# Choosing experts for 29 of 32 tiles inside the last attention step, and loading the projection's weights behind the first keys

## The reference, cut to what matters

```python
x = layernorm(x + self_attention(x))             # 16 heads of 64, causal, then projection and bias
x = layernorm(x + cross_attention(x, ctx, mask)) # 16 heads of 16, 77 keys
logits = x @ Wr.T                                # 8 experts
probs = softmax(logits)
topk_scores, topk_experts = top_k(probs, 2)      # the choice
topk_scores = topk_scores / clip(topk_scores.sum(-1), 1e-9, None)
for e in range(8):                               # in order, with a capacity of 1280 tokens each
    elig = match.any(-1) & ~fallback ; pos = cumsum(elig) - 1
    kept = elig & (pos < cap) ; overflow = elig & (pos >= cap)
    y[kept tokens] += ffn_e(x) * score           # overflow goes to a ninth, fallback FFN
x = layernorm(x + y)
```

## Time and profile before

| | us |
|---|---|
| median of 3 runs | 1583.09 (1582.15 to 1584.85) |
| the profiled execution, whole | 1583.44 |
| its span, first to last instruction | 1581.7 |
| mean granted clock of TensorE | 0.957 |
| busy share of PE, DVE, ACT, POOL | 87%, 78%, 63%, 46% |

### The profile page before, as it was taken

The page is one execution under the profiler, slowest core; times in us unless marked ns, Lnnn a source line. Parts: engine busy times, 40 slices in busy tenths (PEclk is TensorE's granted clock), DMA queues, the critical chain, the costliest instruction groups (busy, mean ns, idle before and its releaser), DMA issues. The chain is left out here.

```text
span 1581.7 us, 49830 instructions
## 1 busy us (share of the span) xinstructions
PE 1382.8 (87%) x17712; PEld 1148.5 (73%) x17712; DVE 1231.6 (78%) x3309; ACT 996.9 (63%) x2381; POOL 731.2 (46%) x921
## 2 busy tenths in 40 slices
PE   3799999999999999999999999882999999999940
PEld 2577888788788878887888888651588888888830
DVE  4889999999999999999989998757555555555538
ACT  3767887788878778777878776522444444444426
POOL 2235456555564575565555634421233344334326
PEclk8899999999999999999999999995799999999985
DMA  8345444344434444443444323108411411111135
GB/s 215 106 130 155 125 130 123 107 138 126 119 95 141 126 115 118 130 124 107 135 124 122 95 81 84 31 8 364 173 55 46 154 46 50 49 49 47 47 118 215
DMA packets 138892, 178.80 MB, mean 113 GB/s; under 512 B 78782, under 2 KB 110654, under 8 KB 134176
## 3 DMA queue, kind: packets, MB, share of 16 engines
q1 hardware_dynamic: 127616, 153.71, 32.5%
q0 software_dynamic: 6816, 17.71, 3.6%
q10 hardware_dynamic: 4224, 4.19, 0.7%
HBM read 93.79 MB, written 65.93 MB: 101 GB/s over the span
## 5 line engine op out<-in xcount | busy, mean ns | idle before, releaser
L1626 PE MATMUL ps_e<-xt,wres 128*128 128x128 f16 x3408 | 354.4, 220 | 0.6 <-issue 0.6
L1626 PEld LDWEIGHTS ps_e<-xt,wres 128*128 x3408 | 287.8, 98 | 72.7 <-issue 1.1
L1682 ACT ACTIVATE act_g<-ps_e,b 128x128 f32<-128x128 f32 x568 | 162.1, 368 | 224.1 <-PE ps_e L1626 113.7
L1633 PE MATMUL ps_e<-wres,g_hi 128*128 x568 | 214.5, 379 | 1.1 <-DVE g_lo L1712 1.1
L691 ACT ACTIVATE probs<-st_k,nmax 128x128 f32<-128x128 f32 (+1 forms) x512 | 200.6, 449 | 13.7 <-DVE nmax L890 11.6
L1585 POOL DMA_INDIRECT z_scr<-e_y,dst_i x71 | 85.0, 1197 | 219.1 <-DVE e_y L1703 215.6
L890 DVE CUSTOM_DVE_ANT_0 st_k<-ps,causal 128x128 f32<-128x128 f32 (+1 forms) x512 | 160.2, 350 | 15.1 <-PE ps L419 14.0
L895 DVE TENSOR_TENSOR pt_lo<-ps,pt_hi 128x384 f16<-128x384 f32 x256 | 141.6, 553 | 17.6 <-ACT pt_hi L698 15.8
L1635 PE MATMUL ps_e<-wres,g_lo 128*128 x568 | 154.8, 273 | 0.0
L427 PE MATMUL ps<-ident,probs 128*128 128x128 f32 x768 | 131.2, 280 | 24.7 <-ACT probs L691 13.8
L1700 DVE SCALAR_TENSOR_TENSOR e_y<-ps_e,b 128x256 f32<-128x256 f32 x71 | 30.2, 425 | 156.0 <-PE ps_e L1635 151.7
(11 more groups left out here) (268 smaller groups left out, 4444.1 us busy)
## 6 DMA issues: line engine op xcount, KB each, us to landing
st_p<-in_moe_w SPq DMA_DIRECT2D x24, 768.0 KB, 5.7
w_scr<-st_p SPq DMA_DIRECT2D x24, 768.0 KB, 4.1
wres<-w_scr SPq DMA_DIRECT2D x18, 1024.0 KB, 19.6
v_scr<-v_tok SPq DMA_DIRECT2D x32, 512.0 KB, 2.6
v_pos<-v_scr SPq DMA_DIRECT2D x32, 512.0 KB, 4.4
k_pair<-k_pair SPq DMA_DIRECT2D x32, 512.0 KB, 4.6
z_scr<-zero SPq DMA_DIRECT2D x32, 256.0 KB, 3.5
wres<-z_scr SPq DMA_DIRECT2D x8, 1024.0 KB, 13.1
```

The lines of the kernel that those rows point to most:

```text
L1626: last = mm(out, w(c * FF + f * P, b, P), xt[:, t % 2, a, c], start=(m == 0), stop=(m == 5))
L1633: mm(out[:, 0:2 * D], g_hi[:, t % G_BUFS, f], w(KC * FF + f * D, 0, 2 * D), start=(f == 0), stop=False, skip_group_check=True)
L1682: nc.scalar.activation(act_g[:, k % 2, f], ps[:, 3 + 2 * (k % 2) + f // 4, (f % 4) * P:(f % 4 + 1) * P], ACT.Gelu, bias=bias[:, f:f + 1], ...
```

## The change

Two edits. The first splits the choice of experts. Logits of tiles 0 to 28 (`EARLY` = 29) exist before step 31; their softmax, their two best experts and their shares are now computed in step 31, at three places of DVE's order (with one `exp` on ACT, and an `iota` on POOL in step 30). The routing block does the same for the last three tiles only, its shares after the packed list, and its `free` is a memset while ACT computes the exponentials. The second takes the projection's two transfers out of `other_weights` and issues them in step -1, after `key_double(0)`; accordingly the 16 pieces of the projection are split after the 8 of the cross-attention, and PE waits for all 24 where it waited for the 24th anyway. Two buffers (`x2_up`, `y2`) move into a staging tile that has become free, and `hot` is allocated earlier.

```diff
+EARLY = TILES - 3
+class Choice:
+    def softmax_in(self, v, link):
+        link(v.tensor_reduce(self.mx, self.lg, AX.X, ALU.max))
+        return v.tensor_tensor(self.pr, self.lg, self.wide(self.mx), ALU.subtract)
+    def softmax_out(self, v, link):
+        link(v.tensor_reduce(self.sm, self.ex, AX.X, ALU.add))
+        link(v.reciprocal(self.mx, self.sm))
+        link(v.tensor_tensor(self.pr, self.ex, self.wide(self.mx), ALU.mult))
+    def best(self, v, link, k):
+        link(v.tensor_reduce(self.m[k], self.pr, AX.X, ALU.max))
+        link(v.tensor_tensor(self.tmp, self.pr, self.wide(self.m[k]), ALU.is_lt))
+        link(v.scalar_tensor_tensor(out=self.tmp, in0=self.tmp, scalar=100.0, in1=ie, op0=ALU.mult, op1=ALU.add))
+        link(v.tensor_reduce(self.ix, self.tmp, AX.X, ALU.min))
+        link(v.tensor_tensor(self.hot[k], ie, self.wide(self.ix), ALU.is_equal))
+        if k == 0:
+            link(v.scalar_tensor_tensor(out=self.pr, in0=self.hot[0], scalar=-4.0, in1=self.pr, op0=ALU.mult, op1=ALU.add))
+    def shares(self, v, link):
+        link(v.tensor_tensor(self.sm, self.m[0], self.m[1], ALU.add))
+        link(v.tensor_scalar(self.sm, self.sm, 1e-9, None, ALU.max))
+        link(v.reciprocal(self.mx, self.sm))
+        for k in range(2):
+            link(v.tensor_tensor(self.w[k], self.m[k], self.mx, ALU.mult))
...
-    SPLITS.append(("p", ld["p"], 32, stage_p[:], [wp[:, k] for k in range(2)], WP_UP))
     for n in ("k", "v", "q", "o"):
         SPLITS.append(("x" + n, ld["x"], 64, stage_x[n][:], [w2[n][:, k] for k in range(2)], WA_UP))
+    SPLITS.append(("p", ld["p"], 32, stage_p[:], [wp[:, k] for k in range(2)], WP_UP))
...
         def other_weights():
-            for half in range(2):
-                sp.dma_start(stage_p[half * HS:(half + 1) * HS], io["proj"].rearrange("(h d) n -> d h n", d=HS)).then_inc(ld["p"], 16)
...
+        def projection():
+            for half in range(2):
+                sp.dma_start(stage_p[half * HS:(half + 1) * HS], io["proj"].rearrange("(h d) n -> d h n", d=HS)).then_inc(ld["p"], 16)
...
                 key_double(s + 1)
+                if s == -1:
+                    projection()
...
-                    pe.wait_ge(s_lo, splits_until("xo"))
+                    pe.wait_ge(s_lo, splits_until("p"))
...
             if has(s - 1):
+                if s == TILES - 1:
+                    act.wait_ge(s_neg, N_SHIFTED)
+                    nc.scalar.activation(early.ex, early.pr, ACT.Exp).then_inc(s_one, 1)
                 stage_c(s - 1, 1)
...
+                if s == TILES - 1:
+                    early_softmax()
                 stage_c(s - 1, 1)
...
+                if s == TILES - 1:
+                    early_best(0)
                 stage_c(s - 1, 3)
...
+                if s == TILES - 1:
+                    early_best(1)
                 stage_c(s - 1, 5)
...
+        def early_softmax():
+            dve.wait_ge(s_lgc, EARLY)
+            link(early.softmax_in(nc.vector, link))
+            dve.wait_ge(s_one, 3)
+            early.softmax_out(nc.vector, link)
+        def early_best(k):
+            dve.wait_ge(s_const, N_CONST + 1)
+            early.best(nc.vector, link, k)
+            if k == 1:
+                early.shares(nc.vector, link)
...
+        late.softmax_in(v, link).then_inc(s_shift, 1)
+        link(v.memset(free[:], 1.0))
         dve.wait_ge(s_exp, 1)
...
+        late.softmax_out(v, link)
         dve.wait_ge(s_const, 10 + PACK)
         for k in range(2):
...
+            late.best(v, link, k)
...
         link(v.tensor_copy(te_pack_i[:], te_pack[:]))
+        late.shares(v, link)
```

More of the change, by code:

```diff
@@ L59, with __init__, wide @@
 K_OPS = OPS_BEFORE[4]
+EARLY = TILES - 3
+class Choice:
+    def __init__(self, lg, hot, w, ex, pr, tmp, mx, sm, m, ix, iota_e):
+        self.lg, self.hot, self.w, self.ex, self.pr, self.tmp = lg, hot, w, ex, pr, tmp
+        self.mx, self.sm, self.m, self.ix, self.iota_e = mx, sm, m, ix, iota_e
+        self.n = lg.shape[1]
+    def wide(self, a):
+        return a.unsqueeze(2).to_broadcast([P, self.n, E])
+    def softmax_in(self, v, link):
[6 more added lines that the diff above has]
+    def best(self, v, link, k):
+        ie = self.iota_e.unsqueeze(1).to_broadcast([P, self.n, E])
+        link(v.tensor_reduce(self.m[k], self.pr, AX.X, ALU.max))
[11 more added lines that the diff above has]
+            link(v.tensor_tensor(self.w[k], self.m[k], self.mx, ALU.mult))
 def attention_block(nc, ctx, io, keep):
@@ L122, in attention_block @@
     ctx_up = sb("ctx_up", [P, KC, CTX], F32)
-    x2_up = sb("x2_up", [P, D], F32)
     x_nat = sb("x_nat", [P, 2, D], F32)
@@ L141, in attention_block @@
     y1 = sb("y1", [P, D], F32)
-    y2 = sb("y2", [P, D], F32)
     stats = sb("stats", [P, 2, 6], F32)
@@ L171, in attention_block @@
     x2_t = stage["v"][:, 0, 0:KC * P].rearrange("p (c t) -> p c t", c=KC)
+    x2_up, y2 = (stage["v"][:, 0, n * D:(n + 1) * D] for n in (1, 2))
     logits = keep["logits"]
@@ L221, in even, with early_rows @@
         return t % 2 == 0
+    N_SHIFTED = 4
+    def early_rows(name, row, at):
+        return stage[name][:, row, at:at + EARLY * E].rearrange("p (t e) -> p t e", e=E)
+    row = stage["v"][:, 1]
+    small = [row[:, 640 + n * TILES:640 + n * TILES + EARLY] for n in range(5)]
+    iota_early = row[:, 640 + 5 * TILES:640 + 5 * TILES + E]
+    early = Choice(logits[:, 0:EARLY * E].rearrange("p (t e) -> p t e", e=E), [keep["hot"][:, k, 0:EARLY] for k in range(2)],
+                   [keep["weights"][:, k, 0:EARLY] for k in range(2)], early_rows("q", 0, 640), early_rows("q", 1, 640), early_rows("k", 0, 768),
+                   small[0], small[1], small[2:4], small[4], iota_early)
     def own(t, cc):
@@ L987, in stage_d @@
                 dve.wait_ge(s_proj2, t + 1)
-                stt(out=y2[:], in0=c7[:, 0:D], scalar=1.0 / (QK_UP * WA_UP), in1=x1[:, p], op0=ALU.mult,
+                stt(out=y2, in0=c7[:, 0:D], scalar=1.0 / (QK_UP * WA_UP), in1=x1[:, p], op0=ALU.mult,
                     op1=ALU.add).then_inc(s_y2, 1)
@@ L999, in second_norm @@
                 dve.wait_ge(s_x2_lo, t - 1)
-            nc.vector.tensor_scalar(x2[:, p], y2[:], mv[:, 1, 0:1], rstd[:, 1:2], ALU.subtract, ALU.mult).then_inc(s_x2, 1)
+            nc.vector.tensor_scalar(x2[:, p], y2, mv[:, 1, 0:1], rstd[:, 1:2], ALU.subtract, ALU.mult).then_inc(s_x2, 1)
         def step(s):
@@ L1107, in fill_own, with link @@
             dve.wait_ge(s_neg, 2)
+        linked = [2]
+        def link(ins):
+            linked[0] += 1
+            ins.then_inc(s_neg, 1)
+            dve.wait_ge(s_neg, linked[0])
+        def early_softmax():
[8 more added lines that the diff above has]
+                early.shares(nc.vector, link)
         nc.vector.memset(sm[:], NEG2).then_inc(s_neg, 1)
@@ L1168, in split_x2 @@
                 pool.wait_ge(s_out_pair[p], 16 * half(t))
-            split(pool, x2[:, p], x2_up[:], x2_pair[:, p, 0], x2_pair[:, p, 1], t, s_x2_hi, s_x2_lo)
+            split(pool, x2[:, p], x2_up, x2_pair[:, p, 0], x2_pair[:, p, 1], t, s_x2_hi, s_x2_lo)
         def split_context(b):
@@ L1250, in _, with number_experts @@
         pool.sem_inc(s_w_lo, 1)
-        run(step, {-1: constants})
+        def number_experts():
+            pool.wait_ge(s_lo, FIRST)
+            nc.gpsimd.iota(iota_early, pattern=[[1, E]], base=0, channel_multiplier=0, allow_small_or_imprecise_dtypes=True).then_inc(s_const, 1)
+        run(step, {-1: constants, TILES - 2: number_experts})
 def weight_rows(io):
@@ L1307, in routing_block @@
     one_row = sb("one_row", [P, T], F32)
[L1308 to L1312, removed]
+    L = T - EARLY
+    mx, sm, ix = (sb("r_" + n, [P, L], F32) for n in ("mx", "sm", "ix"))
+    ex, pr = (sb("r_" + n, [P, L, E], F32) for n in ("ex", "pr"))
+    m = sb("r_m", [P, 2, L], F32)
     tmp = sb("r_tmp", [P, T, E], F32)
-    ix = sb("r_ix", [P, 2, T], F32)
     both = sb("r_both", [P, E, T], F32)
@@ L1326, in routing_block @@
     sk = sb("r_sk", [P, 2, T], F32)
-    w = keep["weights"]
+    late = Choice(lg[:, EARLY:T], [hot[:, k, EARLY:T] for k in range(2)], [keep["weights"][:, k, EARLY:T] for k in range(2)],
+                  ex[:], pr[:], tmp[:, 0:L], mx[:], sm[:], [m[:, k] for k in range(2)], ix[:], iota_e[:])
     si = sb("r_si", [P, 2, T], I32)
@@ L1395, in _ @@
         act.wait_ge(s_shift, 1)
-        nc.scalar.activation(ex[:].rearrange("p t e -> p (t e)"), pr[:].rearrange("p t e -> p (t e)"), ACT.Exp).then_inc(s_exp, 1)
+        nc.scalar.activation(late.ex, late.pr, ACT.Exp).then_inc(s_exp, 1)
         act.wait_ge(s_const, 10 + PACK)
@@ L1433, in wide @@
             return a.unsqueeze(2).to_broadcast([P, T, n])
-        link(v.tensor_reduce(mx[:], lg, AX.X, ALU.max))
-        v.tensor_tensor(pr[:], lg, wide(mx[:]), ALU.subtract).then_inc(s_shift, 1)
+        late.softmax_in(v, link).then_inc(s_shift, 1)
+        link(v.memset(free[:], 1.0))
         dve.wait_ge(s_exp, 1)
```

(9 more changed lines are left out.)

## The result

| | before | changed |
|---|---|---|
| median, runs of one session | 1582.31 us (20 runs) | 1585.28 us (20 runs) |
| ratio, 95% interval | | 1.002 (1.0011 to 1.0028) |
| span of the profiled execution | 1581.7 us | 1584.9 us |
| mean granted clock | 0.957 | 0.959 |
| first scores on PE | 37.81 | 33.10 |

The change made the kernel 3 us slower, where 1.6 us faster was forecast; the time lies just outside the range of 1577 to 1585. The second half of the table (places in the two profiled executions, in us) says where: 4.7 us ahead at the first scores, 3.0 after step 0, 2.4 when step 31 begins, 3.8 behind when the routing begins, 2.5 behind at the experts.

What follows compares the result with a forecast made beforehand. The prediction took PE, then DVE, as fullest on average, with DMA limiting the experts' start. Its terms, -6.2 - 0.3 + 6.0 + 1.0 - 2.1 = -1.6 us, from the median 1583.09 gave 1581.5 us, range 1577 to 1585.

Steps and rivals of the forecast that it cites:

- Step 31, the operations: Step 31: softmax +0.6, best expert +2.6, second best and shares +2.8, together 6.0 us longer (bounds 3 and 7).
- the softmax: Step 31: nothing on DVE, but POOL's `k_bd` and the variance of tile 30 come later, +0.6 us.
- Step 31, the clock: Step 31: two holes of about 2.8 us in PE's work may lower its clock, +1.0 us, between 0 and 3.
- Rival (c): Step 31: clock falls and stays low into step 32, step 31 costs 10.5 in place of 7, total 1585; chance 0.17.
- The start: Before step 0: first keys' doubling issued 6.2 us earlier, -6.2 us, and -0.3 for PE's clock.
- the doubling: Start: transfer of the first keys, issued at 24.33 in place of 30.56, still taking 7.1 us, landing at 31.4.
- the clock term of -0.3: Start: PE resumes at 31.5, just where its clock fell, so -0.3 us taken between 0 and -1.5.
- Rival (d): Start: projection's weights land late, each us beyond 43.9 costs one us of ACT, at 47 total 1584.6; chance 0.08.
- The experts: Routing to experts: choice 3.9 us in place of 9.0, but DMA of weights and biases limits the gain to -2.1 us.
- Rival (a): Step 31: added DVE operations are covered, +2 in place of +7, total 1576.5; chance 0.17.
- (b): Routing to experts: DMA is not next, b2 lands sooner, all 5.3 us count, total 1578.3; chance 0.08.

Runs made afterwards that it cites:

- e1: Kernel before with only the projection's move and the order of its splits, no early choice: 1578.12 us, ratio 0.9968.
- e6: Kernel before with the projection's move, SP waiting for the first keys' doubling to land before asking for the projection's 2 MB: 1580.60 us, ratio 0.999.
- e9: Kernel before with the projection's move and 14 useless matmuls on PE ahead of its wait for the first keys' doubling: 1577.32 us, ratio 0.9969.
- e11: Kernel before with the projection's move alone, repeated on another chip: 1577.60 us, ratio 0.997.
- e2: Changed kernel with the projection's move taken back, so the choice of experts alone: 1589.44 us, ratio 1.0046.
- e4: Changed kernel with the ninth expert's 2.1 MB asked for behind b1 and b2, PE waiting for them only at the ninth expert tile: 1582.65 us, ratio 1.0006.
- e12: Changed kernel run a second time, unaltered: 1584.90 us, ratio 1.0018.
- e5: Changed kernel with 11 useless matmuls on PE in each of the two holes of step 31: 1582.49 us, ratio 1.0004.
- e7: Changed kernel with second best expert moved to step 32 and shares to step 33; softmax and best expert stay in step 31: 1581.70 us, ratio 0.9988.
- e3: Changed kernel with best and second best expert moved into DVE's gaps in step 32, shares to step 33, softmax left in step 31: 1578.16 us, ratio 0.9975.
- e8: Changed kernel with the choice in the gaps of steps 32 and 33 and the ninth expert's weights behind b1 and b2: 1575.19 us, ratio 0.9954.
- e10: Changed kernel with choice in gaps, ninth expert's weights late, 14 useless matmuls at the start, 6 at each of two later holes: 1573.37 us, ratio 0.9947.

## Why the prediction was wrong, point by point

| memset of step 31 to first maxima, us | traces |
|---|---|
| no choice in the last steps | 66.6 (before), 64.8 (e1), 63.3 (e6), 63.3 (e9), 63.3 (e11) |
| all of the choice in step 31 | 72.8 (changed), 73.8 (e2), 74.2 (e4), 73.4 (e12) |
| the same, holes filled | 69.7 (e5) |
| first group in step 31 | 70.2 (e7) |
| in the gaps | 66.9 (e3), 67.9 (e8), 66.4 (e10, with fillers) |

**Step 31, the operations: right.** Forecast 6.0 us. Between traces at full clock it is 69.7 - 63.3 = 6.4. By parts, counted from the memset: PE's first transpose of x comes at 10.98 in e11 and at 12.33 in e12, 1.35 for the softmax (forecast 0.6: the term that was too small); its first score matmul of the second attention (L516 in e11, L568 in e12) at 14.57 and 18.06, 3.5 in all (forecast 3.2).
```profile
1012.55 0.44 PE L492 MATMUL ps<-ident,x 128*128 128x128 f32 x2 [0.18 <-DVE x L940]
1016.14 0.30 PE L516 MATMUL ps<-k_bd,q_hi 128*128 128x308 f16 x1 [0.23 <-DVE q_lo L964]
...
1012.84 0.44 PE L544 MATMUL ps<-ident,x 128*128 128x128 f32 x2 [1.53 <-DVE x L995]
1018.57 0.30 PE L568 MATMUL ps<-k_bd,q_hi 128*128 128x308 f16 x1 [2.73 <-DVE q_lo L1019]
```
(The first two rows are PE of e11, whose memset is at 1001.57; the others PE of e12, memset at 1000.51.)

**Step 31, the clock: the step that failed.** Forecast +1.0 with a bound of 3. The four traces with both holes have a mean of 73.6 us, e5 has 69.7: the clock costs 3.9 there, and 2.8 in the medians. Rival (c) had the fall of the clock, asked for a hole of about 3 us, and gave it 0.17; holes of 2.73 and 2.88 did it. It had the time, 1585, but not the course: the clock didn't stay low into step 32, it came back to 1.00 and fell again. The price was taken too small because the term counted one fall, with 3 us of PE's work behind it. In the changed kernel there are falls behind both holes and one more at 1043 to 1045 (0.50), behind a wait of 1.63 us, and what waits for PE moves with each. That third wait is not the change's: the kernel before has it too (1.62 us, ahead of 1036.92), and the clock falls behind it in before, e1 and the changed kernel, and not in e5, e6, e9 and e11. So a wait of 1.6 us is followed by a fall in some executions and not in others, while behind the hole of 2.73 the clock fell in all five traces that have it. The rule of the Trainium skill that the prediction weighed (page "TensorE: Matmul & The Clock Gate", section "Part 1: The HAM clock gate", where throttled is the default state and activity lifts it) pointed to this end; the sum took the other.

There was a second thing in it, which the trace of before hid. This is the first stretch of step 31 in before, then in e11, the same busy times at another clock:
```profile
1005.58:1013.58 8.00, 7.25 (x87) 6.83 (x88) 4.96 (x17) 3.60 (x9) 0.72 (x2) 0.79 0.01 2
...
1001.57:1009.57 8.00, 7.25 (x100) 7.03 (x101) 4.96 (x17) 3.55 (x9) 2.20 (x3) 1.00 0.01 2
```
It falls twice more in before, to 0.50 at 1040 to 1041 and at 1064 to 1065, and never between the memset and 62 us behind it in e6, e9 and e11. The profiled execution of before took 3.3 us longer from the memset to the maxima than those three did. Comparing it with the changed kernel shows +6.1, which looks like the forecast of the operations exactly; over all traces the choice costs 73.6 - 64.3 = 9.3. Agreement with one trace was luck. In the gaps it is not quite free either: e8, with three falls of the clock as before, needs 67.9 against 66.6. The 1.3 us are about what the softmax costs, and the softmax stayed in step 31.

**The start: right in kind, too large by 1.4 us.** Forecast -6.5, measured -5.1 (0.9968) and -4.7 (0.997). The 5.1 us lie between the medians' 4.1 for e1 and 5.2 for e11. The queue behaved as forecast (v landed after 2.7 us, the first keys' doubling issued at 24.2 to 25.6, and the first scores at 31.5 to 32.3 in six of the eleven traces). The term that was mis-sized is the doubling: the prediction kept its 7.1 us because v_in lay beside it before as well, and left out that the 2 MB now lie right behind it. Its mean of 8.1 against 6.9 is 1.2 of the missing 1.4 to 1.8; e6, made to show that, paid for it at the other end, so its share of the median is not isolated. Nor is the clock term of -0.3: the granted clock fell to 0.50 behind this wait in every trace but that of e10. Rival (d) didn't happen in the changed kernel, but e6 shows how near it was: asking 6 us later is enough.

**The experts: right mechanism, gain 1.4 in place of 2.1.** The six traces with the early choice and the weights in the changed kernel's order have the token copy 52.0 to 52.3 us behind the maxima, against 53.4 to 53.9. The prediction put it at the last packet of b2, 51 us behind the maxima. In the changed kernel's trace the last packets of that queue land at 1127.2 to 1128.0, 51.3 to 52.0 us behind them, and the copy begins within 1 us; why the transfers end later than the 51 us of before is open. The choice took 4.4 us and not 3.9, 0.6 of it a wait for POOL's constants that had been covered before; it costs nothing, since the DMA is later.

**The sum.** With what the parts measured alone, -5.1 + 7.3 = +2.2, and +2.8 (e12) to +3.2 by the ratios for both together: they add up within their intervals. Rival (a) fell with e7, where neither group was covered, and (b) with e4, where the DMA was next. The forecast had -6.5 + 4.9. Of the 4.6 us between -1.6 and +3.0, the start is 1.4, the experts 0.7, and the other 2.5 step 31, nearly all of it the clock.

## What to carry to other kernels

Work added to an engine is covered only where that engine was waiting for another anyway and nobody waits for its next result sooner; look for the gaps of the adding engine that end on someone else (here DVE in step 32 of the kernel before: 3.8 and 2.6 us), not for a low busy share. Two holes of 2.7 and 2.9 us cut into TensorE's stream came with 6.4 us of added work on the chain here, and cost 2.8 us (medians) to 3.9 us (traces) on top, because the granted clock fell behind them. When two kernels are compared by one trace each, count the clock's falls in both before a difference is put down to the change: here they were worth 3.3 us in a stretch of 65.

## What the runs showed of the hardware

- Matmuls without a use, in the place of idleness, gave back 2.8 us (e5), and the granted clock of the whole stretch was 1.00, where it fell to 0.50 three times. At the start 14 of them changed the median by 0.3 us (e9 against e11).
- The granted clock fell behind the hole of 2.73 us in five traces of five, and behind one of 1.6 us in some traces and not in others.
- The same SBUF to SBUF transfer of 512 KB took 6.7 to 7.1 us alone and 7.0 to 9.6 with 2 MB asked for right behind it, in two groups (seven traces up to 7.9, four from 9.2).
- The times of one kernel's executions mostly spread over 4 to 8 us (changed: 1581.4 to 1588.5), and the slower ones have the lower mean granted clock (correlation -0.66 in the 20 of the changed kernel, -0.76 in the 12 of e12). The places of the clock's falls differ between them: before, e4 and e10 have 0.79 in the first 8 us of step 31, the other traces 1.00, though PE has the same work there.
- At the start the row can show a granted clock of 1.00 while matmuls take nearly double: two of 128x512 took 1.01 us at 18.15 in the changed kernel and 0.59 at 18.20 in before. Full speed began between 14.3 us (e7) and 22.8 us (e1), and v of tile 0 was issued some 1.2 us later in the two executions where it began latest (the changed kernel at 21.8, and e1).
